# Signals and maxima of the maximum scores, per bank of two heads instead of per four heads

## The chip, the cores and the metric

The kernel runs on one core of a Trainium2 chip. The metric is the device time of one execution in microseconds (us), lower is better. A core has five engines that run their own instruction streams and meet only through semaphores: TensorE (PE; its weight loads are shown apart as PEld), VectorE (DVE), ScalarE (ACT), GpSimd (POOL) and SyncE (SP), which here issues all DMAs.

## The reference, cut to what matters

The kernel computes one block of a gated cross-attention network on x (4 x 2048 x 512) with a context of 154 tokens per batch item:

```python
x = x + tanh(g_xattn) * xattn(layernorm(x), ctx)      # 16 heads of 32, softmax over the 154 context tokens
x = x + tanh(g_ffn) * ffn(layernorm(x))               # 512 -> 2048 -> 512, relu, float_quantize of hidden, w2, out
```

Inside the attention, `att = q k^T / sqrt(32)`, a softmax over 154 columns, `y = att v`, and a projection by `Wo`. The softmax subtracts a maximum per row and head, and that maximum is what the change is about.

## The kernel before, in words

The 8192 rows of x are worked in 16 chunks of 512 rows (`CHUNK`), each with 4 tiles of 128 rows (`TILES`). The program is a software pipeline written out by hand: every stage has a table of beats (`MAX_AT`, `Q_AT`, `HIDDEN_AT`, ...), a chunk begins every 28 beats, and the first chunks have tables of their own (`MAX_OWN`, ...). Each engine walks over the same beats and issues, in a fixed order, its part of every stage that is due. Nothing is reordered at run time; each engine takes its stream in order.

The stages that matter here:

- **q projection** (`query`, L532, 12 matmuls `ring<-xT,wq`): PE writes one group of four heads (m = 0 to 3) to a ring bank of PSUM. DVE moves it out (`query_out`, L1091), ACT rounds it to f16 (`query_hi`, L883), POOL makes the low part (L1194).
- **rank** (PE, L638): for chunk c and u = 4m + t, two matmuls of 128 rows by 308 columns give the coarse scores of tile t against 154 keys of heads 4m to 4m+3. Each matmul covers two heads and fills one bank of the two-bank tile `m_ps` (for four early u of chunk 0, `PAIRED`, it is `s_ps`). Only the second signals `scored`. Before a rank, PE waits on `maxed` until the maximum of the rank before it has been taken, since both use the same two banks.
- **row_max** (DVE, L1048): one reduction over both banks, 616 columns to 4 maxima (`smax`), signals `maxed`.
- **shift** (DVE, L1054, L1059): after 8 ranks the maxima are scaled, rounded and transposed; SP writes them as an extra row of `qstack`, so that the exact scores come out shifted.
- **lift** (PE, L661 for the 26 left-over keys, L668 for the 128 main keys of a head): the exact scores, exponentiated twice by ACT (L834 as f16, L837 as f32); POOL forms the difference (L1182). `value` (L685 to L700) makes denominators and y.
- **projection, hidden layer, output** (L532 with `wo,yT` and `late_a,w`; L745): the bulk of PE's time. Between chunks, transposes of x run as DMAs on SP (L371, L381).

With 16 chunks of 16 ranks there are 256 ranks and 256 maxima. On PE the ranks stand singly between the 12-matmul products in the steady part, and close together while the pipeline fills. In the excerpt below, `rank` and `row_max` are the two sides; `keys_diagonal` (SP), `query_hi` (ACT) and `lift_ready` (PE) also wait on the two semaphores, and `shift` on `maxed`.

Of the kernel before, what the change touches and what calls it, by code (L numbers as in the profile page):

```python
# [10 lines left out]
ALU = mybir.AluOpType  # L11
ACT = mybir.ActivationFunctionType
AX = mybir.AxisListType
ABSMAX = bass.bass_isa.ReduceOp.absmax

P = 128
# [3 lines left out]
GH = P // DH  # L20
HID = 2048
HT = HID // P
TILES = 4
# [89 lines left out]
PAIRED = {(0, 1), (0, 3), (0, 5), (0, 7)}  # L113
# [3 lines left out]
def build(nc, x, ctx_t, g_xattn, g_ffn, wq_t, bq, wk_t, bk, wv_t, bv, wo_t, bo, w1_t, b1, w2_t, b2, out):  # L117
    NB, NK = ctx_t.shape[2], ctx_t.shape[3]
    NCH = x.shape[0] // CHUNK
    CPB = NCH // NB  # L120
# [3 lines left out]
    HK = 2 * NK  # L124
# [3 lines left out]
    with ExitStack() as es:  # L128
        def sb(name, shape, dt):
            return es.enter_context(nc.sbuf_tensor(name, shape, dt))  # L130

        def sem(name):
            return es.enter_context(nc.semaphore(name))
# [9 lines left out]
        kblk = sb("kblk", [P, KT, GH * NK], F16)  # L143
# [9 lines left out]
        qparts = sb("qparts", [P, 2, KT, CHUNK], F16)  # L153
# [19 lines left out]
        smax = sb("smax", [P, 2, 2 * GH, TILES], F32)  # L173
# [60 lines left out]
        def score_banks(c, u):  # L234
            return s_pair if (c, u) in PAIRED else m_ps
# [18 lines left out]
        q_done, q_moved, q_hi, q_lo = sem("q_done"), sem("q_moved"), sem("q_hi"), sem("q_lo")  # L254
        scored, maxed, negated, shifted = sem("scored"), sem("maxed"), sem("negated"), sem("shifted")
# [14 lines left out]
        ident_done, turned, turn_moved = sem("ident_done"), sem("turned"), sem("turn_moved")  # L270
# [65 lines left out]
        def unit(c, m, u):  # L336
            return group(c, m) * (GH + 1) + u

        def q_stage(c, m):
            if c:  # L340
                return q32[:]
            return (p32[:, 0, :], p32[:, 1, :], q32[:], y32[:])[m]
# [15 lines left out]
        def _(sp):  # L358
# [49 lines left out]
                    sp.dma_start(row[:, a], negT[32 * a:32 * a + 32, pair, :]).then_inc(shift_in[pair], DMA)  # L408

            def keys_diagonal(b, k):  # L410
                sp.wait_ge(scored, b * CPB * 16)
                if b == 2:
                    sp.wait_ge(kv_lo, EARLY + KT)
                for h in range(GH):
                    sp.dma_start(kblk[DH * h:DH * h + DH, :, h * NK:(h + 1) * NK],
                                 kst[DH * h:DH * h + DH, 0, :, b * NK:(b + 1) * NK]).then_inc(kblk_in, DMA)
# [87 lines left out]
            for beat in range(FIRST, (NCH - 1) * PERIOD + LAST):  # L504
                once(lambda pair: q_out(0, pair), QUERY_ROWS_AT, beat)
                once(lambda pair: q_in(0, pair), QUERY_ROWS_AT, beat)
                once(lambda b: values_stacked(b, 0), VALUE_ROWS_AT, beat)
                run(lambda c, t: x_load(c, t) if c > 1 else None, XLOAD_AT, beat)
                run(turn_x2, X2TURN_AT, beat, X2TURN_OWN)
                run(shift_row, SHIFT_AT, beat, SHIFT_OWN)  # L510
                run(lambda c, t: turn_x(c, t) if c else None, XTURN_AT, beat, XTURN_OWN)
                run(left_out, LEFT_AWAY_AT, beat)
                run(left_in, LEFT_BACK_AT, beat)
                run(reload, RELOAD_AT, beat, RELOAD_OWN)
                run_batch(keys_diagonal, KBLK_AT, beat)
                run_batch(values_stacked, VBLK_AT, beat)
                run(lambda c, pair: q_out(c, pair) if c else None, STACK_OUT_AT, beat, STACK_OUT_OWN)
                run(lambda c, pair: q_in(c, pair) if c else None, STACK_IN_AT, beat, STACK_IN_OWN)
                once(keys_out_all, KEYS_OUT_AT, beat)
                run_batch(keys_stacked, KST_AT, beat)  # L520
                run(store, STORE_AT, beat, STORE_OWN)
                once(w2_load, W2_LOAD, beat)
# [4 lines left out]
        def _(pe):  # L527
# [94 lines left out]
            def rank(c, u):  # L622
                m, t = divmod(u, TILES)
                pe.wait_ge(q_hi, c * KT + m + 1)
                if (c, u) == (0, 0):
                    pe.wait_ge(turn_moved, TILES)
                elif (c, u) == (0, 1):
                    pe.wait_ge(q_moved, 2)
                elif (c, u - 1) in PAIRED or (c, u) in PAIRED:
                    pe.wait_ge(maxed, c * 16 + u - 1)  # L630
                else:
                    pe.wait_ge(maxed, c * 16 + u)
                if c == 0 and u % 8 == 0:
                    pe.wait_ge(kblk_set[u // 8], GH)
                elif u == 0 and c >= CPB:
                    pe.wait_ge(kblk_in, c // CPB * GH * DMA)
                for half in range(2):
                    last = pe.matmul(score_banks(c, u)[:, half, 0:HK], qparts[:, 0, m, t * P:t * P + P],  # L638
                                     kblk[:, m, half * HK:(half + 1) * HK], start=True, stop=True)
                last.then_inc(scored, 1)  # L640

            def lift_ready(c, m, u):

                n = unit(c, m, u)
                if n >= 2:
                    pe.wait_ge(exped, n - 1)
                else:
                    pe.wait_ge(maxed, len(PAIRED) * 2)
                if m % 2 == 0 and u == 0:
                    pe.wait_ge(stack_in[m // 2], (c + 1) * 2 * STACK * DMA)  # L650
                    pe.wait_ge(shift_in[m // 2], (c + 1) * 4 * DMA)
                    if c < CPB:
                        pe.wait_ge(kcat_set, (m // 2 + 1) * GH)
                    else:
                        pe.wait_ge(kcat_in[m // 2], c // CPB * 2 * STACK * DMA)

            def lift_left(c, m):
                lift_ready(c, m, 0)
                dst = s_ps[unit(c, m, 0) % 2]
                for h in range(GH):  # L660
                    last = pe.matmul(dst[DH * h:DH * h + DH, :], kcat[0:97, GH * m + h, P:KW],  # L661
                                     qstack[0:97, GH * m + h, :], start=True, stop=True)
                last.then_inc(lifted, 1)
# [93 lines left out]
            for beat in range(FIRST, (NCH - 1) * PERIOD + LAST):  # L757
                run(lift_left, LEFT_AT, beat)
                run(value, VALUE_AT, beat)
                run(lift_main, MAIN_AT, beat)  # L760
                run(rank, MAX_AT, beat, MAX_OWN)
                once(stack_keys, KSTACK_AT, beat)
                steps_of(Q_STEPS, first_query, beat)
                steps_of(KV_STEPS, keys_values, beat)
                run(lambda c, m: query(c, m) if c else None, Q_AT, beat, Q_OWN)
                run(project, O_AT, beat, O_OWN)
                once(hidden_half, HIDDEN_HALVES, beat)
                run(lambda c, j: hidden(c, j) if c or j > 1 else None, HIDDEN_AT, beat, HIDDEN_OWN)
                run(ffn_out, FFN_AT, beat, FFN_OWN)

        @block.scalar
        def _(act):
# [105 lines left out]
            def query_hi(c, m):  # L878
                act.wait_ge(q_moved, c * KT + m + 1)
                if c:  # L880
                    act.wait_ge(scored, (c - 1) * 16 + 4 * m + 4)
                    act.wait_ge(stack_in[m // 2], c * 2 * STACK * DMA)
                nc.scalar.copy(qparts[:, 0, m, :], q_stage(c, m)).then_inc(q_hi, 1)  # L883

# [17 lines left out]
            for n in range(2):  # L902
                keys_values(n)
            query_hi(0, 0)
            first_blocks(0)
            query_hi(0, 1)
            for beat in range(FIRST, (NCH - 1) * PERIOD + LAST):
                run(exp_left, LEFT_AT, beat)
# [18 lines left out]
        def _(dve):  # L927
# [114 lines left out]

            def row_max(c, u):
                m, t = divmod(u, TILES)
                dve.wait_ge(scored, c * 16 + u + 1)
                heads = slice(m % 2 * GH, m % 2 * GH + GH)
                scores = score_banks(c, u)[:, :, 0:HK].rearrange("p a (h k) -> p a h k", h=2)
                nc.vector.tensor_reduce(smax[:, m // 2, heads, t].rearrange("p (a h) -> p a h", a=2), scores,  # L1048
                                        AX.X, ALU.max).then_inc(maxed, 1)

            def shift(c, pair):
                n = 2 * c + pair
                dve.wait_ge(maxed, c * 16 + 8 * pair + 8)
                nc.vector.tensor_scalar(neg16[:], smax[:, pair].rearrange("p h t -> p (h t)"), -1.0 / SHIFT, None, ALU.mult  # L1054
                                        ).then_inc(negated, 1)
                dve.wait_ge(negated, n + 1)
                if c:
                    dve.wait_ge(shift_in[pair], c * 4 * DMA)
                nc.vector.transpose(negT[:, pair, :], neg16[:]).then_inc(shifted, 1)  # L1059
# [254 lines left out]
```

## Time and profile before

| what | value |
|---|---|
| median of 3 runs | 1573.12 us (1571.85 to 1573.48) |
| the profiled execution | 1575.78 us, its span 1573.9 us |
| mean granted clock of TensorE in it | 0.992 |
| PE busy | 1528.2 us (97%), 8600 matmuls |
| DVE busy | 802.0 us (51%), 1299 instructions |
| ACT busy | 818.8 us (52%) |
| POOL busy | 879.2 us (56%) |

The profiled execution lies 2.66 us above the median of the runs; 1.9 us of it lie outside the span. Busy time is time in which at least one instruction of the engine was in flight. A matmul's shown duration is longer than the time until the next one may start, because matmuls are pipelined: what PE can do is read from the distance between starts. Slices of the span show PE at nine tenths or more from 160 us on; before that the pipeline fills and the weights are prepared.

### The profile page before, as it was taken

The numbers are of one execution on the slowest core, as the hardware profiler recorded it, in microseconds if no ns is written. First come the engines' busy times: TensorE is split into PE (matmuls) and PEld (weight loads), VectorE is DVE, ScalarE is ACT, GpSimd is POOL, SyncE is SP. The second block draws the span as 40 slices with busy tenths as digits, with TensorE's granted clock in tenths as the row PEclk, the third lists the DMA queues.
The fourth block names the chain that finished last, engine by engine and source line by source line (L and its number), as shares of the span: only waits on it lengthen the run. The fifth ranks groups of instructions, "written<-read, shape, count | busy, mean of one in ns | idle before, by whom it ended". The sixth has DMA issues, their size and how long they took to land.

```text
span 1573.9 us, 23573 instructions
## 1 busy us (share of the span) xinstructions
PE 1528.2 (97%) x8600; PEld 696.7 (44%) x8600; DVE 802.0 (51%) x1299; ACT 818.8 (52%) x1202; POOL 879.2 (56%) x919
## 2 busy tenths in 40 slices
PE   7877999999999999999999999999999999999998
PEld 4333444444444444444444444444444444444443
DVE  7777364555635455564645556464555646434221
ACT  5755755545455454545546454544645454455421
POOL 3778474654746465474646547464654747445310
PEclk9989999999999999999999999999999999999999
DMA  8446463454434353354444434344444434333120
GB/s 332 110 148 159 162 133 112 134 127 110 121 114 104 124 125 114 105 121 127 111 127 122 115 107 120 113 109 137 126 115 108 123 109 108 99 101 87 44 54 27
DMA packets 252854, 186.69 MB, mean 119 GB/s; under 512 B 160012, under 2 KB 209476, under 8 KB 251076
## 3 DMA queue, kind: packets, MB, share of 16 engines
q1 hardware_dynamic: 252740, 185.19, 42.7%
q8 instruction: 69, 1.13, 0.3%
q14 instruction: 45, 0.37, 0.1%
HBM read 99.95 MB, written 51.59 MB: 96 GB/s over the span
## 4 chain that ended last, share of the span: by engine, by line
PE 91%; SPq 2%; DVE 2%; DMA 2%; ACT 1%; issue 1%; POOL 1%; ACTq 0%; DVEq 0%
PE ring L532 62%; PE ring L745 14%; PE m_ps L638 4%; PE s_ps L668 3%; PE y_ps L696 2%; PE d_ps L685 2%; PE s_ps L661 1%; DMA resid<-in_wo_t 1%; PE y_ps L700 1%; PE d_ps L688 1%; SPq L371 1%; DVE smax L1048 0%; SPq L381 0%; PE ring L574 0%; ACT p L837 0%
## 5 line engine op out<-in xcount | busy, mean ns | idle before, releaser
L532 PE MATMUL ring<-late_a,w 128*128 128x512 f16 (+1 forms) x3096 | 703.9, 378 | 5.6 <-DMA late_a<-x 4.0
L532 PEld LDWEIGHTS ring<-late_a,w 128*128 128x128 f16 x3096 | 302.2, 98 | 346.2 <-issue 11.5
L859 ACT ACTIVATE late_b<-ring,b_sb,wsc 128x512 fp8e4<-128x512 f32 x256 | 199.3, 779 | 434.7 <-PE ring L532 434.7
L1182 POOL TENSOR_TENSOR pmain<-p,pmain 128x512 f16<-128x512 f32 x256 | 308.4, 1209 | 167.8 <-ACT p L837 167.6
L1048 DVE TENSOR_REDUCE smax<-m_ps 128x4 f32<-128x616 f32 x252 | 200.9, 797 | 244.7 <-PE m_ps L638 244.6
L837 ACT ACTIVATE p<-s_ps,prob_log,sc 128x512 f32<-128x512 f32 x320 | 248.0, 775 | 1.5 <-POOL pmain L1182 0.6
L745 PE MATMUL ring<-w,late_b 128*128 128x512 fp8e4 x1024 | 228.2, 379 | 0.9 <-ACT late_b L859 0.9
L834 ACT ACTIVATE pmain<-s_ps,prob_log,sc 128x512 f16<-128x512 f32 x256 | 198.3, 775 | 7.7 <-PE s_ps L668 7.7
L1182 POOL TENSOR_TENSOR pleft<-p,pleft 128x512 f16<-128x512 f32 x64 | 77.2, 1206 | 193.0 <-ACT p L837 192.8
L532 PE MATMUL ring<-wo,yT 128*128 128x512 f16 x768 | 174.5, 381 | 0.0
L532 PE MATMUL ring<-xT,wq 128*128 128x512 f16 x720 | 169.0, 385 | 2.2 <-DVE x L1030 2.2
L745 PEld LDWEIGHTS ring<-w,late_b 128*128 128x128 fp8e4 x1024 | 99.9, 98 | 122.3 <-ACT late_b L859 1.4
L1091 DVE TENSOR_SCALAR q<-ring,sc,bias_s 128x512 f32<-128x512 f32 x61 | 49.4, 810 | 171.1 <-PE ring L532 170.9
L1194 POOL TENSOR_TENSOR qparts<-q,qparts 128x512 f16<-128x512 f32 x61 | 72.6, 1190 | 96.6 <-ACT qparts L883 94.6
L638 PE MATMUL m_ps<-kblk,qparts 128*128 128x308 f16 x504 | 109.0, 298 | 16.2 <-DVE smax L1048 13.9
L532 PEld LDWEIGHTS ring<-wo,yT 128*128 128x128 f16 x768 | 74.1, 98 | 88.9 <-DVE resid L1114 5.7
L532 PEld LDWEIGHTS ring<-xT,wq 128*128 128x128 f16 x720 | 71.1, 99 | 83.7 <-issue 5.5
L1081 DVE TENSOR_TENSOR ffn<-ring,bq 128x512 f16<-128x512 f32 x64 | 44.1, 689 | 117.3 <-PE ring L745 117.3
L668 PE MATMUL s_ps<-qstack,kcat 97*128 97x512 f16 x256 | 95.6, 386 | 4.5 <-ACT p L837 4.4
L876 ACT CAST x<-xn 128x512 f16<-128x512 f32 x64 | 39.5, 617 | 114.9 <-DVE xn L1123 112.0
L1208 POOL TENSOR_TENSOR x<-xn,x 128x512 f16<-128x512 f32 x64 | 80.8, 1262 | 31.3 <-ACT x L876 31.2
L883 ACT CAST qparts<-q 128x512 f16<-128x512 f32 x61 | 37.7, 618 | 112.2 <-DVE q L1091 112.1
(158 smaller groups left out, 1452.7 us busy)
## 6 DMA issues: line engine op xcount, KB each, us to landing
qstack<-q_rows SPq DMA_DIRECT2D x192, 128.0 KB, 3.0
pstack<-left_rows SPq DMA_DIRECT2D x192, 128.0 KB, 2.6
xin<-in_x SPq DMA_DIRECT2D x64, 256.0 KB, 3.4
q_rows<-qparts SPq DMA_DIRECT2D x32, 512.0 KB, 2.8
left_rows<-pleft SPq DMA_DIRECT2D x64, 256.0 KB, 2.5
resid<-in_x SPq DMA_DIRECT2D x64, 256.0 KB, 3.2
out_x<-resid SPq DMA_DIRECT2D x64, 256.0 KB, 2.6
resid<-in_w_t SPq DMA_DIRECT2D x5, 1024.0 KB, 5.4
```

The lines of the kernel that those rows point to most:

```text
L532: last = pe.matmul(dst, lhs(a, k), rhs(b, k), start=(k == 0 and p == 0), stop=(k == n_k - 1 and p == 2))
L638: last = pe.matmul(score_banks(c, u)[:, half, 0:HK], qparts[:, 0, m, t * P:t * P + P], kblk[:, m, half * HK:(half + 1) * HK], start=True, ...
L668: pe.matmul(s_ps[unit(c, m, 1 + h) % 2], kcat[0:97, GH * m + h, 0:P], qstack[0:97, GH * m + h, :], start=True, stop=True).then_inc(lifted, 1)
L745: last = pe.matmul(ring_bank("f", c, t)[:], hT[:, j, t * P:t * P + P], w2[:, j, :], start=(j == 0), stop=(j == HT - 1))
L834: nc.scalar.activation(dst, s_ps[n % 2], ACT.Exp, bias=prob_log[:, 0:1], scale=sc[:, 7:8])
L837: nc.scalar.activation(p32[:, n % 2, :], s_ps[n % 2], ACT.Exp, bias=prob_log[:, 0:1], scale=sc[:, 7:8]).then_inc(exped, 1)
L859: nc.scalar.activation(hT[:, j, :], ring_bank("h", c, j)[:], ACT.Relu, bias=b1_sb[:, j:j + 1], scale=wsc[:, j // 4, 1:2], saturate=False). ...
L1048: nc.vector.tensor_reduce(smax[:, m // 2, heads, t].rearrange("p (a h) -> p a h", a=2), scores, AX.X, ALU.max).then_inc(maxed, 1)
L1091: nc.vector.tensor_scalar(q_stage(c, m), ring_bank("q", c, m)[:], sc[:, 6:7] if c else sc[:, 5:6], bias_s[:, m:m + 1], ALU.mult, ALU.add). ...
L1182: nc.gpsimd.tensor_tensor(part[:, 1, :], p32[:, n % 2, :], part[:, 0, :], ALU.subtract).then_inc(prob_lo, 1)
L1194: nc.gpsimd.tensor_tensor(qparts[:, 1, m, :], q_stage(c, m), qparts[:, 0, m, :], ALU.subtract).then_inc(q_lo, 1)
L1208: nc.gpsimd.tensor_tensor(x2_16[:, t % 2, 1, :], xn2[:], x2_16[:, t % 2, 0, :], ALU.subtract).then_inc(x2_split, 1)
```

## The change

The pair of matmuls of a rank now signals twice, once per bank, and DVE takes two maxima of 308 columns, each released by its own bank's signal, each signalling `maxed`. PE's first matmul of a rank waits for the first half of the maximum before it, the second matmul for the second half. All other waits on the two semaphores keep their meaning: their numbers are doubled.

```diff
@@ keys_diagonal (SP)
-                sp.wait_ge(scored, b * CPB * 16)
+                sp.wait_ge(scored, 2 * b * CPB * 16)
@@ rank (PE)
-                if (c, u) == (0, 0):
-                    pe.wait_ge(turn_moved, TILES)
-                elif (c, u) == (0, 1):
-                    pe.wait_ge(q_moved, 2)
-                elif (c, u - 1) in PAIRED or (c, u) in PAIRED:
-                    pe.wait_ge(maxed, c * 16 + u - 1)
-                else:
-                    pe.wait_ge(maxed, c * 16 + u)
...
                 for half in range(2):
-                    last = pe.matmul(score_banks(c, u)[:, half, 0:HK], qparts[:, 0, m, t * P:t * P + P],
-                                     kblk[:, m, half * HK:(half + 1) * HK], start=True, stop=True)
-                last.then_inc(scored, 1)
+                    if (c, u) == (0, 0):
+                        pe.wait_ge(turn_moved, TILES)
+                    elif (c, u) == (0, 1):
+                        pe.wait_ge(q_moved, 2)
+                    elif (c, u - 1) in PAIRED or (c, u) in PAIRED:
+                        pe.wait_ge(maxed, 2 * (c * 16 + u - 1) - 1 + half)
+                    else:
+                        pe.wait_ge(maxed, 2 * (c * 16 + u) - 1 + half)
+                    pe.matmul(score_banks(c, u)[:, half, 0:HK], qparts[:, 0, m, t * P:t * P + P],
+                              kblk[:, m, half * HK:(half + 1) * HK], start=True, stop=True).then_inc(scored, 1)
@@ lift_ready (PE)
-                    pe.wait_ge(maxed, len(PAIRED) * 2)
+                    pe.wait_ge(maxed, len(PAIRED) * 4)
@@ query_hi (ACT)
-                    act.wait_ge(scored, (c - 1) * 16 + 4 * m + 4)
+                    act.wait_ge(scored, 2 * ((c - 1) * 16 + 4 * m + 4))
@@ row_max (DVE)
-                dve.wait_ge(scored, c * 16 + u + 1)
-                heads = slice(m % 2 * GH, m % 2 * GH + GH)
-                scores = score_banks(c, u)[:, :, 0:HK].rearrange("p a (h k) -> p a h k", h=2)
-                nc.vector.tensor_reduce(smax[:, m // 2, heads, t].rearrange("p (a h) -> p a h", a=2), scores,
-                                        AX.X, ALU.max).then_inc(maxed, 1)
+                for half in range(2):
+                    heads = slice(m % 2 * GH + 2 * half, m % 2 * GH + 2 * half + 2)
+                    dve.wait_ge(scored, 2 * (c * 16 + u) + half + 1)
+                    nc.vector.tensor_reduce(smax[:, m // 2, heads, t],
+                                            score_banks(c, u)[:, half, 0:HK].rearrange("p (h k) -> p h k", h=2),
+                                            AX.X, ALU.max).then_inc(maxed, 1)
@@ shift (DVE)
-                dve.wait_ge(maxed, c * 16 + 8 * pair + 8)
+                dve.wait_ge(maxed, 2 * (c * 16 + 8 * pair + 8))
```

No instruction of PE moves; what changes there is which of them wait. PE, where the ranks of chunk 1 stand close together (`m_ps<-kblk,qparts` is a rank, `s_ps<-qstack,kcat` a lift), before:

```order
L668 MATMUL s_ps<-qstack,kcat 128x512 [waits exped]
L638 MATMUL m_ps<-kblk,qparts 128x308 [waits maxed,q_hi]
L638 MATMUL m_ps<-kblk,qparts 128x308
L638 MATMUL m_ps<-kblk,qparts 128x308 [waits maxed,q_hi]
L638 MATMUL m_ps<-kblk,qparts 128x308
```

The same place after the change:

```order
L667 MATMUL s_ps<-qstack,kcat 128x512 [waits exped]
L638 MATMUL m_ps<-kblk,qparts 128x308 [waits maxed,q_hi]
L638 MATMUL m_ps<-kblk,qparts 128x308 [waits maxed]
L638 MATMUL m_ps<-kblk,qparts 128x308 [waits maxed,q_hi]
L638 MATMUL m_ps<-kblk,qparts 128x308 [waits maxed]
```

Every second matmul of a rank now waits too. DVE at the same place (the rows behind the first are the three, then one, maxima of these ranks, with a layer-norm statistic between), before:

```order
L1107 TENSOR_SCALAR xin<-xin,mv,rs 128x512 [waits ln1_rs]
L1048 TENSOR_REDUCE smax<-m_ps 128x4 [waits scored] x3
L1097 BN_STATS bns<-xin 128x6 [waits ln1_stats,x_in2]
L1099 BN_AGGR mv<-bns 128x2 [waits ln1_bn]
L1048 TENSOR_REDUCE smax<-m_ps 128x4 [waits scored]
```

After the change:

```order
L1107 TENSOR_SCALAR xin<-xin,mv,rs 128x512 [waits ln1_rs]
L1047 TENSOR_REDUCE smax<-m_ps 128x2 [waits scored] x6
L1097 BN_STATS bns<-xin 128x6 [waits ln1_stats,x_in2]
L1099 BN_AGGR mv<-bns 128x2 [waits ln1_bn]
L1047 TENSOR_REDUCE smax<-m_ps 128x2 [waits scored] x2
```

Three maxima have become six and one has become two; nothing else stands elsewhere.

## Rows read from the trace of the kernel before

**Rows 1.** Who waited for whom on PE: us in total, times, longest

```profile
PE m_ps L638 <- DVE smax L1048: 13.9, 11, 3.4
```

**Rows 2.** Busy time by stretch: stretch, its length, then PE, PEld, DVE, ACT, POOL, clock, DMA

```profile
400.00:800.00 400.00, 400.00 (x2291) 181.75 (x2290) 212.15 (x340) 207.22 (x309) 239.27 (x251) 1.00 0.45 117
800.00:1200.00 400.00, 400.00 (x2319) 181.92 (x2318) 203.18 (x324) 212.53 (x317) 230.10 (x238) 1.00 0.43 118
```

**Rows 3.** Instructions on tile m_ps: count, ns min/median/max, first and last start

```profile
L638 PE MATMUL m_ps<-kblk,qparts x504: 291/295/462, 28.1 to 1414.7; 128*128 128x308 f16 x168
L1048 DVE TENSOR_REDUCE smax<-m_ps x252: 768/801/804, 28.5 to 1415.0; 128x4 f32<-128x616 f32 x126
```

**Rows 4.** Groups of instructions of DVE by shape: count, us in total, mean ns

```profile
L941 DVE TENSOR_REDUCE mag<-w 128x1 f32<-128x2048 f32 x1 | 2.3, 2286 | 0.0
```

**Rows 5.** Instructions of DVE in order of time: start us, duration us, instruction

```profile
40.00 0.95 DVE L1000 TENSOR_REDUCE kblk<-kst 32x308 f16<-32x308 f16 x2
...
830.79 0.79 DVE L1048 TENSOR_REDUCE smax<-m_ps 128x4 f32<-128x616 f32 x1
831.50 0.68 DVE L1097 BATCH_NORM_STATS2 bns<-xin 128x6 f32<-128x512 f32 x1
```

**Rows 6.** Instructions of PE in order of time, steady part, around 813 us

```profile
813.20 0.38 PE L668 MATMUL s_ps<-qstack,kcat 97*128 97x512 f16 x1
813.42 0.43 PE L638 MATMUL m_ps<-kblk,qparts 128*128 128x308 f16 x2
813.68 2.75 PE L532 MATMUL ring<-xT,wq 128*128 128x512 f16 x12
816.27 0.43 PE L638 MATMUL m_ps<-kblk,qparts 128*128 128x308 f16 x2
```

**Rows 7.** Instructions in order of time around 308 us, and the last such place

```profile
308.22 0.79 DVE L1048 TENSOR_REDUCE smax<-m_ps 128x4 f32<-128x616 f32 x1
308.79 0.38 PE L668 MATMUL s_ps<-qstack,kcat 97*128 97x512 f16 x1
309.15 0.42 PE L638 MATMUL m_ps<-kblk,qparts 128*128 128x308 f16 x2
...
1317.55 0.42 PE L638 MATMUL m_ps<-kblk,qparts 128*128 128x308 f16 x2
```

**Rows 8.** DVE, ACT and PE in order of time while the pipeline fills

```profile
105.00 0.79 DVE L1048 TENSOR_REDUCE smax<-m_ps 128x4 f32<-128x616 f32 x1
106.39 0.80 DVE L1048 TENSOR_REDUCE smax<-m_ps 128x4 f32<-128x616 f32 x1 [0.61 <-PE m_ps L638]
...
109.53 0.78 ACT L837 ACTIVATE p<-s_ps,prob_log,sc 128x512 f32<-128x512 f32 x1
...
105.93 0.42 PE L638 MATMUL m_ps<-kblk,qparts 128*128 128x308 f16 x2 [3.40 <-DVE smax L1048]
107.34 0.67 PE L638 MATMUL m_ps<-kblk,qparts 128*128 128x308 f16 x2 [0.98 <-DVE smax L1048]
109.00 0.67 PE L638 MATMUL m_ps<-kblk,qparts 128*128 128x308 f16 x2 [0.56 <-DVE smax L1048]
110.65 0.67 PE L638 MATMUL m_ps<-kblk,qparts 128*128 128x308 f16 x2 [0.56 <-DVE smax L1048]
...
111.55 5.28 PE L532 MATMUL ring<-xT,wq 128*128 128x512 f16 x12
116.66 0.43 PE L638 MATMUL m_ps<-kblk,qparts 128*128 128x308 f16 x2
```

**Rows 9.** Busy time by stretch, 110 to 115 us, columns as in the second group

```profile
110.00:115.00 5.00, 4.44 (x13) 1.65 (x13) 4.90 (x8) 4.87 (x6) 4.92 (x4) 0.50 0.10 32
```

**Rows 10.** The chain of work that ended last, in order of time: start us, us, what

```profile
39.29 0.79 DVE smax L1048
...
123.94 1.19 SPq L371
...
152.88 2.43 DMA late_a<-x
```

**Rows 11.** Instructions of PE in order of time, the last wait for a maximum

```profile
219.78 0.42 PE L638 MATMUL m_ps<-kblk,qparts 128*128 128x308 f16 x2 [0.98 <-DVE smax L1048]
```

## The prediction

> **What bounds the kernel now.** I read three views in this order. First the busy time by stretch: from 400 to 1200 us PE is busy without a gap at full granted clock, while DVE is busy half the time [rows 2]. In that part only what lies between two starts on PE counts. Second, who PE waited for: for the maxima it waited 13.9 us in 11 places, which is all this change can touch directly [rows 1]; the last of them is at 219.78 us [rows 11]. So the visible waits all belong to the filling of the pipeline. Third, the instructions in order of time, for waits too short to show as idle. One such repeats: at 308.79 us a lift of 512 columns starts, and the rank behind it starts 0.36 us later, where the same pair of rows is 0.22 us apart elsewhere [rows 6, 7]. The maximum before it ended at 308.22 + 0.79 = 309.01, and the rank follows by 0.14. That is a loss of 0.13 us per chunk, 12 times from 309.15 to 1317.55 [rows 7].
>
> **Prices.** PE's pair of 308 columns takes 0.26 us from start to next start, 0.13 per matmul [rows 6]. One matmul lasts 295 ns until its end is seen [rows 3]; DVE starts 0.46 us after the start of a pair (105.93 to 106.39), so 0.33 after that of its first matmul. PE starts 0.15 us after the end of a maximum (106.39 + 0.80 to 107.34) [rows 8].
> A maximum of 616 columns lasts 801 ns [rows 3], one of 2048 columns 2286 ns [rows 4]: (2286 - 801)/1432 = 1.04 ns a column and 0.16 us fixed. A half therefore lasts 0.16 + 308 x 1.04 ns = 0.48 us. Its successor starts 0.08 us before its end (830.79 + 0.79 against 831.50, [rows 5]), so two halves are about 0.39 us apart and both take 0.39 + 0.48 = 0.87 us, against 0.80. That is my value. The dearer end is the one pair of reductions of 308 elements in the trace: 0.95 us for two [rows 5]; with 0.48 for one they did not overlap, and both halves would take 0.95 to 0.98 us. It is another form (32 partitions, SBUF to SBUF), so I keep it for the range and take the overlap of the row on the same tile.
>
> **What a wait becomes.** Three cases.
> (a) DVE is late, PE's pair was finished long ago. Before, the next pair is through 0.80 + 0.15 + 0.26 = 1.21 us after DVE starts. After, the second matmul starts at 0.39 + 0.48 + 0.15 = 1.02 and is through at 1.15: 0.06 us won. The halves help little, since the second matmul waits for the second half, and PE had only 0.13 us to do in between. At the dearer end it is 0.05 lost.
> (b) DVE waits for PE. Before: 0.46 + 0.80 + 0.15 + 0.26 = 1.67 us from pair to end of the next pair. After: 0.33 + 0.39 + 0.48 + 0.15 + 0.13 = 1.48, so 0.19 won, 0.08 at the dearer end.
> (c) The same at half clock, where the pairs are 1.66 us apart [rows 8]: 0.47 for the pair instead of 0.26. Before 1.66 + 0.47 = 2.13; after 0.47 + 0.39 + 0.48 + 0.15 + 0.23 = 1.72, so 0.41 won; the lift between two pairs (0.43 at this clock) fits into the wait.
>
> **The filling, part by part.** The pair at 105.93 is case (a), 107.34 case (b), 109.00 and 110.65 case (c): 0.06 + 0.19 + 0.41 + 0.41 = 1.07 us. But the lift between 110.65 and 111.55 also waits for ACT, which ends an exponential at 109.53 + 0.78 = 110.31 [rows 8]; the product at 111.55 can then come no earlier than 110.31 + 0.15 + 0.43 = 110.89. So 0.66 us are left, and I take 0.7 with what a few earlier waits give. The product's end at 116.66 releases the chain that goes on, so this gain is kept. Waits behind it, up to 155 us, are worth nothing: from 123.94 us the chain is SP's queue of transposes and the DMA at 152.88 [rows 10]. The same holds before 66 us, except that a few maxima lie on the chain, the last of a row at 39.29 us [rows 10]: two of them each cost 0.07 more, a third, case (a) or (b), gives some back: +0.1 us. The wait at 219.78 [rows 11] is case (a): -0.06.
>
> **The steady part.** The 12 hidden waits are case (a): 12 x 0.06 = 0.7 us won, 0.6 lost at the dearer end. DVE gets 0.07 us more work per rank, 16 x 0.07 = 1.1 us in a chunk of 92 us with half of DVE idle [rows 2]: I cost it at nothing, its cover is that idle time; where it is missing (DVE late in front of something PE wants), it is 0.07 us a maximum. PE gets 256 more waits and 256 more signals. A lift has one of each: it takes 0.22 us, a matmul of the same width inside a product 2.59/12 = 0.216 [rows 6], so a wait with its signal costs 0 to 0.01 us; I take 0.004: 256 x 0.004 = 1.0 us, with 0 and 2.6 as ends. ScalarE's and SP's doubled counts change nothing.
>
> **Sum.** -0.7 (filling) + 0.1 (early chain) - 0.06 (219.78) - 0.7 (12 waits) + 1.0 (waits and signals) = -0.4 us, so 1575.4 us against the profiled execution's 1575.78. The median of the runs is 2.66 us lower: 1573.12 - 0.4 = 1572.7 us. A measurement of this kernel can tell about 0.2%, 3.1 us, from no change: I forecast no change.
>
> **A rule against the trace.** The maximum fits a fixed part of 0.16 us plus 1.04 ns a column, but its successor starts before its end [rows 3 to 5]. The Trainium skill, VectorE: DVE Perf Modes, section "The DRAIN you can't avoid", says that the next op does not start until the pipe is empty, and its rules for authors advise fewer ops. By that rule the two halves take 0.96 us, every case (a) turns into a loss of 0.03 us, and my sum would be +0.7. The trace disagrees for neighbours of this instruction: 0.71 us between starts at 0.79 us duration.
>
> **Rivals.**
> 1. *DVE becomes the bound of the filling* (slower). Mechanism: the second half starts only after the first has ended and the signal is back, and each maximum on DVE's stretches (100 to 116 us and around 40 us) delays what PE and the DMAs wait for. It decides against the change from 0.45 us between the halves on (then case (a) gains nothing). Price: 2 x 0.49 - 0.71 = 0.27 us more per maximum; if the 24 maxima of chunk 0's second half and chunk 1 all lie on the path, 6.5 us, with 12 x 0.05 of the steady part and 1 us of waits 8.1: 1581 us. For it: the 0.95 us row. Against: DVE waits for PE in most of these places, and the neighbours overlap. Chance 0.06 for more than 3.1 us.
> 2. *Every further signal holds PE up* (slower). Mechanism: the pair is no longer back to back. The widest reading of the rows is a tear as long as a round to the other engine, 0.15 us [rows 8], 256 x 0.15 = 38 us: 1611 us; the nearest row allows 0.01 us, 2.6 us. Against: lifts carry a wait and a signal each and follow at 0.22 us. Chance 0.05. The Trainium skill, TensorE: Matmul & The Clock Gate, section "The cost: per-tile semaphore tail", gives 26.3 ns for each further increment, one behind the other; as an estimate from that page it would be 256 x 26.3 ns = 6.7 us, 1578.4 us with the rest of my sum. No row here shows such a tail.
> 3. *The clock turns the filling* (faster). The product at 111.55 takes 5.11 us to 116.66 at half clock (granted 0.50, [rows 9]), 2.59 at full clock [rows 6], after PE had been idle 3.40 us at 105.93. If the shorter waits bring the clock back before it, 2.5 us more are won, 1573.12 - 0.4 - 2.5 = 1570.2 us; with one more such product in the filling, 1567.7. Against: the idle 3.40 us in front remain, only 0.1 us shorter. Chance 0.12, of which about 0.04 lie within 3.1 us. It can go the other way as well (a product pushed to half clock), with 2.5 us and 0.04 of chance, mostly within 3.1 us.
> 4. *It doesn't split anything*: excluded, since the order of the built program shows two reductions and two waits per rank.
>
> **How the numbers follow.** No change (sum -0.4) 0.73; rival 1 0.06 beyond the bound; rival 2 0.05; rival 3 0.12, and 0.04 for its mirror. Faster by over 0.2%: 0.08 of rival 3 and 0.02 for gains that I capped: 0.10. Slower by over 0.2%: 0.06 + 0.05 + 0.01 = 0.12. Within: 0.78. Range: the low end takes rival 3's first step, 1570.2; the high end all dearer ends, +0.1 + 0.05 + 0.6 + 2.6, with no gain in the filling: +3.35, 1576.5. I give 1570.2 to 1576.3.
>
> **What would show it.** Right: halves of 0.47 to 0.49 us, 0.39 apart where DVE is late; DVE busy up by 15 to 20 us; PE's waits for the maxima down from 13.9 to some 8 to 11 us; at the 12 places 0.30 us instead of 0.36 between lift and end of wait, or a small gap inside the pair; the pair still 0.26 to 0.27 us in the steady part; chunk period unchanged to 0.1 us. Wrong: pairs 0.30 us or longer everywhere (rival 2), halves 0.48 apart or more (rival 1), granted clock above 0.50 from 110 to 115 us (rival 3).

## The result, and the profile after

Before and after, run alternately on one chip: 1572.22 us median before (13 runs, 1568.03 to 1573.93), 1568.14 us after (13 runs, 1566.59 to 1571.01). The ratio is 0.9978 with a 95% interval of 0.997 to 0.9985: 3.5 us (2.4 to 4.7) faster, where gains in us, here and below, are worked out from the ratio and the median of before (the two medians alone differ by 4.1 us). The forecast was 0.4 us; the lower end of its range, 1570.2 us, lay 2.1 us above the 1568.14 us. Of these 2.1 us, 0.9 are the kernel before, whose median is now 1572.22 instead of the 1573.12 that the forecast started from: taken as a difference the lower end was 2.9 us faster, inside the interval of what was measured. The profiled execution of the change took 1567.14 us, its span is 1565.2 us.

The page after the change, its head and the engines' busy time:

```profile
span 1565.2 us, 23829 instructions
PE 1524.9 (97%) x8600; PEld 696.1 (44%) x8600; DVE 819.9 (52%) x1555; ACT 818.1 (52%) x1202; POOL 878.0 (56%) x919
```

DVE has 256 instructions more and 17.9 us more work, as costed (0.07 us for each of 256 maxima). The busy times of ACT and POOL stand as they did, to within 0.3%. Who PE waited for, after the change (us in total, times, longest):

```profile
PE m_ps L638 <- DVE smax L1047: 8.6, 9, 2.4
PE m_ps L638 <- issue: 2.6, 2, 2.4
```

The 13.9 us of [rows 1] have become 8.6 in the row for the maxima; 2.6 more are put down to nothing, so the row alone says little of what was won. The instructions on tile m_ps after the change (count, ns min/median/max, first and last start):

```profile
L638 PE MATMUL m_ps<-kblk,qparts x504: 291/295/457, 27.4 to 1406.0; 128*128 128x308 f16 x168
L1047 DVE TENSOR_REDUCE smax<-m_ps x504: 447/471/483, 27.8 to 1406.6; 128x2 f32<-128x308 f32 x168
```

A half takes 471 ns, forecast 480 ns from the fit through [rows 3, 4].

**The steady part.** The clearest measure is the distance between chunks. The transposes of the denominators on DVE come four to a chunk; the first one of chunk 3 and the first one of chunk 14 are 11 chunks apart. Before:

```profile
326.76 0.70 DVE L1068 STREAM_TRANSPOSE y<-d_ps 128x512 f32<-128x512 f32 x1
1335.16 0.70 DVE L1068 STREAM_TRANSPOSE y<-d_ps 128x512 f32<-128x512 f32 x1
```

After:

```profile
319.58 0.70 DVE L1068 STREAM_TRANSPOSE y<-d_ps 128x512 f32<-128x512 f32 x1
1326.52 0.70 DVE L1068 STREAM_TRANSPOSE y<-d_ps 128x512 f32<-128x512 f32 x1
```

1008.40/11 = 91.67 us before, 1006.94/11 = 91.54 us after, and each of the eleven distances is within 0.01 us of its mean. So 0.13 us a chunk are won, all of the hidden wait of [rows 7], 12 x 0.13 = 1.6 us. From the first transpose of chunk 14 to the end it is 238.7 us in all fourteen profiles of this document, so what else differs between two of them lies in the filling. The same place after the change, in order of time:

```profile
301.17 0.85 DVE L1047 TENSOR_REDUCE smax<-m_ps 128x2 f32<-128x308 f32 x2
301.75 0.38 PE L667 MATMUL s_ps<-qstack,kcat 97*128 97x512 f16 x1
301.97 0.43 PE L638 MATMUL m_ps<-kblk,qparts 128*128 128x308 f16 x2
302.08 0.10 PEld L638 LDWEIGHTS m_ps<-kblk,qparts 128*128 128x128 f16 x1 [0.23 <-DVE smax L1047]
302.24 2.75 PE L532 MATMUL ring<-wo,yT 128*128 128x512 f16 x12
```

The two halves end at 301.17 + 0.85 = 302.02, 0.85 us after they began, 0.06 more than one whole maximum took. The rank follows the lift by 0.22 us, without a wait; the second matmul's weights are loaded at 302.08, 0.06 us after the second half, and the next product comes 0.27 us after the pair, as anywhere. Reckoned with the 0.15 us of the forecast, the second matmul would have come at 302.17.

**The filling** went 7.2 us faster in this pair of profiles (326.76 to 319.58). That is more than the runs bear out: the profiled execution of before (1575.78 us) took longer than any of the 13 runs. What repeats in other profiles is told below.

### The profile page after: what moved, and what is told of

Read it like the earlier page. It is cut to its first block, busy times and chain, and to the rows that moved or that the text cites. A ratio compares the mean times of both kernels' runs of the same rounds, so it can differ in the third digit from the quotient of the medians.

```text
span 1565.2 us, 23829 instructions
## 1 busy us (share of the span) xinstructions
PE 1524.9 (97%) x8600; PEld 696.1 (44%) x8600; DVE 819.9 (52%) x1555; ACT 818.1 (52%) x1202; POOL 878.0 (56%) x919
## 4 chain that ended last, share of the span: by engine, by line
PE 92%; DVE 2%; DMA 2%; SPq 1%; ACT 1%; POOL 1%; issue 1%; ACTq 0%; DVEq 0%
PE ring L532 62%; PE ring L744 14%; PE m_ps L638 4%; PE s_ps L667 3%; PE y_ps L695 3%; PE d_ps L684 2%; PE s_ps L660 1%; DMA resid<-in_wo_t 1%; PE y_ps L699 1%; PE d_ps L687 1%; DVE smax L1047 0%; PE ring L574 0%; ACT p L836 0%; PE ring L592 0%; ACT pmain L833 0%
## 5 line engine op out<-in xcount | busy, mean ns | idle before, releaser
L1047 DVE TENSOR_REDUCE smax<-m_ps 128x2 f32<-128x308 f32 x504 | 217.2, 473 | 219.4 <-PE m_ps L638 218.9
L1203 POOL TENSOR_TENSOR x<-xin,x 128x512 f16<-128x512 f32 x60 | 69.2, 1154 | 48.0 <-ACT x L867 48.0
```

Of the source, the lines that this page charges most:

```text
L1047: nc.vector.tensor_reduce(smax[:, m // 2, heads, t], score_banks(c, u)[:, half, 0:HK].rearrange("p (h k) -> p h k", h=2), AX.X, ALU.max).t ...
L1203: nc.gpsimd.tensor_tensor(x16[:, t % 2, 1, :], xin[:, t, :], x16[:, t % 2, 0, :], ALU.subtract).then_inc(x_split, 1)
```

## The experiments

The kernels were timed in three groups of four (1 to 4, 5 to 8, 9 to 12), each group alternately with the kernel before on one chip. In the diffs, `split(c)` says whether chunk c works by halves, and `signals(n)` is the number of signals of the first n ranks.

**1 and 2: halves in the steady part alone, halves in the filling alone.** The change, but `split` true for chunks 3 to 15, or for chunks 0 to 2:

```diff
+        def split(n):
+            return n >= 3        # e2: n < 3
...
                 for half in range(2):
+                    if half == 0 or split(c):
... (the waits of the change, counted with signals)
-                last.then_inc(scored, 1)
+                    if half or split(c):
+                        last.then_inc(scored, 1)
```

(against the kernel before, PE's side; DVE takes two maxima where `split(c)` holds). Where a chunk is not split, the rank and its maximum are those of before, but for one rank: the first one behind a split chunk, (3, 0) in e2 and (1, 0) in e10 below, waits for the first half of the maximum before it alone, for both its matmuls. To be safe it would have to wait for both halves; it is one rank of 256.

> Theory A (the halves take away waits on PE: 12 hidden ones of 0.13 us in the steady part, the shown ones in the filling; waits and signals themselves cost nothing): with halves only from chunk 3 on, the 12 places vanish, the distance between chunks is 91.54 us instead of 91.67, and the total is 1.6 us lower (ratio 0.999). Theory B (the gain is all in the filling, where the granted clock and the queue of transposes happen to fall better): no change, ratio 1.000, distance between chunks 91.67 us.

> Halves only in chunks 0 to 2. Theory A: the rest of the gain, some 2 to 2.5 us (ratio 0.9985), distance between chunks as before the change, 91.67 us. Theory B: the whole gain, 3.5 to 4 us (ratio 0.9976).

Measured: e1 0.9989 (0.998 to 0.9998), 1.7 us faster, distance between chunks 91.54 us. e2 0.9993 (0.9983 to 1.0003), 1.1 us faster, 91.67 us. So theory B falls: about half of the gain is the steady part, and it is the hidden waits. The gain of e2 is not clear of zero (2.7 us faster to 0.5 slower). The two add up to 2.8 us; the full change was measured three times, at 3.5, 2.8 and 3.3 us.

**3: PE waits for the whole maximum.** From the full change (in its own counts, the ranks around `PAIRED` likewise):

```diff
-                        pe.wait_ge(maxed, 2 * (c * 16 + u) - 1 + half)
+                        pe.wait_ge(maxed, 2 * (c * 16 + u))
```

> Both signals and both maxima in all chunks, but PE's first matmul of a rank waits for the whole maximum before it. Theory A (what pays is that the first matmul needs only the first half): the two maxima take 0.05 to 0.06 us longer than one, so the 12 hidden waits grow from 0.13 to about 0.19 us and the distance between chunks to about 91.72 us; the filling keeps only what DVE wins by starting 0.13 us earlier; total between 0.5 us slower and 1 us faster. Rival C (what pays is DVE's earlier start): nearly the whole gain, ratio 0.998.

Measured: 1.0014 (1.0005 to 1.0023), 2.2 us slower (0.8 to 3.6); from the starts at 325.39 and 1334.46 us the distance between chunks is 91.73. The hidden wait, in order of time:

```profile
306.78 0.85 DVE L1058 TENSOR_REDUCE smax<-m_ps 128x2 f32<-128x308 f32 x2
307.36 0.38 PE L677 MATMUL s_ps<-qstack,kcat 97*128 97x512 f16 x1
307.78 0.42 PE L646 MATMUL m_ps<-kblk,qparts 128*128 128x308 f16 x2
```

Lift to rank is 0.42 us instead of 0.36: the 0.06 us by which two halves take longer, as theory A had it for the steady part. In twelve chunks that makes 0.7 us. The total is worse than theory A's 0.5 us, so some 1.5 us are lost in the filling; no run shows by what. Rival C falls in any case: DVE's earlier start by itself is not what pays.

**4: both maxima start late.**

```diff
-                    dve.wait_ge(scored, 2 * (c * 16 + u) + half + 1)
+                    dve.wait_ge(scored, 2 * (c * 16 + u) + 2)
```

> Both signals and both maxima, PE waits by halves, but both maxima wait for the second matmul of the rank. Theory A: the steady part as with the full change (DVE is late there anyway), distance between chunks 91.54 us, 1.6 us; in the filling each wait in which DVE waits for PE gives 0.06 us instead of 0.19, so 0.5 to 1 us less than the full change: total 2.5 to 3.5 us lower. Rival C: the gain goes, ratio 1.000.

Measured: 0.9982 (0.9973 to 0.9991), 2.8 us faster, distance between chunks 91.54 us. As theory A had it. With experiment 3 it shows that the first matmul's earlier release carries the whole gain of the steady part (91.73 to 91.54 us) and most of the total (3 and 4 differ from the full change by one edit each).

**5: the price of signals and waits.** PE's side alone; DVE takes one maximum:

```diff
                 for half in range(2):
+                    if half and c * 16 + u > 1:
+                        pe.wait_ge(maxed, c * 16 + u - (1 if (c, u - 1) in PAIRED or (c, u) in PAIRED else 0))
-                    last = pe.matmul(score_banks(c, u)[:, half, 0:HK], qparts[:, 0, m, t * P:t * P + P],
-                                     kblk[:, m, half * HK:(half + 1) * HK], start=True, stop=True)
-                last.then_inc(scored, 1)
+                    pe.matmul(score_banks(c, u)[:, half, 0:HK], qparts[:, 0, m, t * P:t * P + P],
+                              kblk[:, m, half * HK:(half + 1) * HK], start=True, stop=True).then_inc(scored, 1)
...
-                dve.wait_ge(scored, c * 16 + u + 1)
+                dve.wait_ge(scored, 2 * (c * 16 + u + 1))
```

> PE's side of the change alone: each matmul of a rank signals, the second one waits too (for the same whole maximum as the first, so it never holds), DVE takes one maximum as before. The term of the sum says 0.004 us a rank: distance between chunks 91.67 + 16 x 0.004 = 91.73 us, total +1.0 us. Theory A' (a satisfied wait and a signal cost nothing): 91.67 us, ratio 1.000. Rival 2 of the prediction as the page's figure has it, 26 ns a signal: 92.09 us, +6.7 us.

Measured: 1.0003 (0.9992 to 1.0013), and the two transposes:

```profile
323.32 0.70 DVE L1069 STREAM_TRANSPOSE y<-d_ps 128x512 f32<-128x512 f32 x1
1331.65 0.70 DVE L1069 STREAM_TRANSPOSE y<-d_ps 128x512 f32<-128x512 f32 x1
```

1008.33/11 = 91.67 us. 16 further signals and 16 further satisfied waits a chunk cost less than 0.01 us together. The 1.0 us of the sum was nothing. The program has no instruction more either: its page counts 23573 instructions, as before.

**6: one semaphore instead of two in front of a rank.** From the kernel before:

```diff
-                pe.wait_ge(q_hi, c * KT + m + 1)
+                if t == 0:
+                    pe.wait_ge(q_hi, c * KT + m + 1)
```

(at t > 0 PE has already waited for the same value at t = 0).

> The kernel before with one edit: PE waits for the rounded queries only at the first tile of a group, so a rank at t > 0 waits for one semaphore instead of two. Theory D (a second semaphore in front of a matmul makes it start some 0.05 us later once the maximum is there; this is why the hidden waits vanished wholly): the 12 hidden waits fall from 0.13 to 0.08 us, distance between chunks 91.62 us, total 0.6 us lower. If the number of semaphores does not matter: 91.67 us and 1.000.

Measured: 0.999 (0.9976 to 1.0004), distance between chunks 91.59 us, 0.08 less than before. The hidden wait:

```profile
303.65 0.79 DVE L1066 TENSOR_REDUCE smax<-m_ps 128x4 f32<-128x616 f32 x1
304.23 0.38 PE L678 MATMUL s_ps<-qstack,kcat 97*128 97x512 f16 x1
304.49 0.11 PEld L647 LDWEIGHTS m_ps<-kblk,qparts 128*128 128x128 f16 x2 [0.38 <-DVE smax L1066]
304.50 0.44 PE L647 MATMUL m_ps<-kblk,qparts 128*128 128x308 f16 x2
```

The maximum ends at 304.44, PE starts 0.06 us later, not 0.14 as in [rows 7]. Theory D holds, and with more than it asked: a second semaphore in front of the matmul costs 0.08 us at the moment of release. The page counts 23381 instructions, 192 fewer than before, one for each rank at t > 0: a second wait on a matmul is an instruction of its own, a single one is not. Whether the order of the two waits matters was not tried. The whole kernel's gain of 1.6 us (interval to 0.6 us slower) can't be told from the 0.08 x 12 = 1.0 us that this makes.

**7 and 8: the full change with that edit, and the full change again.**

> The full change with the same edit. In the steady part nothing is left to win: 91.54 us. By theory D each of the some ten waits of the filling gets up to 0.05 us shorter: 0 to 0.5 us below the full change, ratio to before 0.9975 to 0.998.

> The full change once more, with the numbers of the semaphores computed by a function and the same instructions and waits: distance between chunks 91.54 us, 3 to 4 us below before, ratio 0.9978; beside it the other runs of this call can be read.

Measured: e7 0.9993 (0.9981 to 1.0005), e8 0.9982 (0.9971 to 0.9992), both 91.54 us between chunks. Theory D's further gain did not show; e7 lies 1.7 us above e8, none of it in the steady part, and its waits for the maxima are shorter (7.7 us against 8.4). The intervals of the two overlap, so it isn't shown that e7 is worse; shorter waits in the filling did at least not bring a filling that is shorter by their amount.

**9 to 12: which chunks of the filling.** `split(n)` as `n >= 1`; as `n == 0`; `n >= 1` with the single wait from chunk 1 on; and the full change a third time.

> Halves from chunk 1 on; the ranks before 74 us are as before the change. In the traces so far, every kernel whose early ranks are released sooner shows half clock from 66.5 to about 70 us behind the wait for pstack, and its second denominator transpose comes 0.7 to 1.9 us later than the first, against before; in the kernels with chunk 0 as before it does not. Theory E (that dip is caused by the shorter waits of chunk 0, whose gain is hidden behind SP's queue anyway, and costs 1 us): full clock from 62 to 72 us, the gain at 100 to 117 us kept, total 1 us below the full change, ratio to before 0.9972. If the early shift does not matter in the end: as the full change, 0.998.

> Halves in chunk 0 alone. Theory E: granted clock 0.83 or lower from 62 to 72 us, nothing won, total 0.5 to 1 us above before, ratio 1.0003 to 1.0007, distance between chunks 91.67 us. If the dip has another cause: ratio 1.000 and clock 1.00.

> As the kernel with halves from chunk 1, and from chunk 1 on PE waits for the rounded queries only at the first tile of a group. Theory D gives up to 0.3 us more than that kernel (ratio 0.9970); the earlier kernel with the single wait everywhere was 1 to 2 us worse than the full change, which theory D does not explain: if this one is worse too, shorter waits in the filling are not worth what they take off.

> The full change once more beside these: ratio to before 0.998, clock below 1.00 from 62 to 72 us, distance between chunks 91.54 us.

| kernel | ratio to before (95%) | median us | granted clock, 62 to 72 us |
|---|---|---|---|
| e9, halves from chunk 1 | 0.9970 (0.9959 to 0.9981) | 1567.20 | 1.00 |
| e10, chunk 0 only | 1.0007 (0.9997 to 1.0016) | 1572.53 | 1.00 |
| e11, from chunk 1, one wait | 0.9969 (0.9956 to 0.9983) | 1567.85 | 1.00 |
| e12, the full change | 0.9979 (0.9967 to 0.9990) | 1568.24 | 0.83 |

Chunk 0 gives nothing that shows, so the filling's gain comes from chunks 1 and 2. Between e9 and e11 the single wait makes no difference, so the loss that e7 seemed to have is not repeated. The ratios stand in the order that theory E gave, with its sizes, but their intervals overlap, and e10's clock speaks against it: its early ranks are released as in the full change, PE waits 1.85 us for `pstack`, and it ran on at full clock. Busy time of two stretches of 2 us (stretch, length, PE, PEld, DVE, ACT, POOL with their instructions, PE's granted clock, share of DMA, GB/s); first the change, whose PE had idled 1.89 us before 65.92 us,

```profile
66.00:68.00 2.00, 2.00 (x28) 0.80 (x27) 1.13 (x3) 0.62 (x2) 2.00 (x3) 0.69 0.44 68
68.00:70.00 2.00, 2.00 (x8) 0.94 (x5) 1.25 (x2) 0.00 (x0) 1.35 (x2) 0.50 0.50 22
```

then e10, idle 1.85 us before 66.05:

```profile
66.00:68.00 2.00, 1.95 (x29) 1.04 (x30) 1.00 (x3) 0.78 (x2) 2.00 (x3) 1.00 0.28 55
68.00:70.00 2.00, 1.69 (x8) 0.71 (x6) 1.97 (x4) 1.22 (x2) 1.53 (x2) 1.00 0.74 49
```

Nine profiles have the release of the maxima changed in chunk 0, and in eight of them the clock fell to half here, in e10's not; in the five with chunk 0 as before it fell in none. The length of this one idle stretch does not tell the two apart: half clock came with 1.39 us (e3), 1.43 (e6) and 1.65 to 1.89 us, full clock with 1.36 to 1.49 us (before, e1, e5, e9, e11) and 1.85 us (e10). In the change, 0.69 and 0.50 over 4 us leave 1.6 us of full clock ungranted. Whether e9 is really better than the full change is open; it is not worse.

## Why the prediction was wrong

**What held.** PE is the bound of the steady part and DVE's extra work is hidden there. The size of a half (0.471 for 0.48 us), the overlap (0.85 for 0.87 us for both), the 12 hidden waits, and that PE waits there for a late maximum. Rivals 1 and 2 did not come: the halves overlap, and 256 signals cost nothing. The rule that was set against the trace had been read too widely: the same section of the Trainium skill (VectorE: DVE Perf Modes, "The DRAIN you can't avoid") goes on that a next op that is not held starts earlier, and the trace agrees: two halves of 0.47 us take 0.85 us together. Three steps failed, two in the steady part and one in the filling.

**Step 1, "the second matmul starts at 0.39 + 0.48 + 0.15 = 1.02".** The 0.15 us from the end of a maximum to PE was read on ranks that wait for two semaphores. The second matmul of a rank waits for `maxed` alone, and follows by 0.06 us (302.02 to 302.08). Experiment 6 shows the same on its own: 0.06 instead of 0.14 us, 91.59 instead of 91.67. With it, case (a) wins 0.06 + 0.09 = 0.15 us instead of 0.06, more than the 0.13 that there was: 1.6 us instead of 0.7. Case (b) wins 0.28 instead of 0.19: the wait of [rows 11] was one of these (the pair before it started at 218.37 and the maximum 0.46 us later), not case (a) as I had put it. Before, 220.04 - 218.37 = 1.67 us from that pair to the end of the next; after:

```profile
211.63 0.43 PE L638 MATMUL m_ps<-kblk,qparts 128*128 128x308 f16 x2
212.59 0.60 PE L638 MATMUL m_ps<-kblk,qparts 128*128 128x308 f16 x2 [0.53 <-DVE smax L1047]
213.02 1.24 PE L532 MATMUL ring<-wo,yT 128*128 128x512 f16 x5
```

213.02 - 211.63 = 1.39 us (the view ends at 214 us, within the product).

What neither the forecast nor the change touches is why DVE is late there. Before the change, around the hidden wait of [rows 7]:

```profile
306.85 1.16 POOL L1182 TENSOR_TENSOR pmain<-p,pmain 128x512 f16<-128x512 f32 x1
306.92 1.37 DVE L1107 TENSOR_SCALAR xin<-xin,mv,rs 128x512 f32<-128x512 f32 x1 [2.80 <-POOL rs L1220]
```

The last step of the layer norm takes 1.37 us, 0.52 at 319.26 us, and only then comes the maximum, at 308.22. So it is in all 12 places: 1.37 us, begun 0.07 us after the start of an instruction of POOL's on pmain and ended 0.28 us after that one's end. With 0.52 us, as an estimate, the maximum would end 0.85 us earlier, before the lift even starts, and the change would have nothing to win in the steady part. No kernel was made that tries it.

**Step 2, "a wait with its signal costs 0.004 us".** The term of 1.0 us was mis-sized: it came from a difference of two rounded starts (0.22 against 0.216), and experiment 5 measures nothing. Both steps together: forecast +0.3 us for the steady part, measured -1.6 (experiment 1: -1.7). That is 1.9 of the 3.1 us by which I was off; the other 1.2 are the filling. With these two steps right the sum would have been -2.3 us, 1570.8 us, inside the range.

**Step 3, the filling: "0.66 us are left, this gain is kept".** Forecast -0.7; the three measurements of the full change less 1.6 leave 1.2 to 1.9 us, experiment 2 has 1.1 (0.5 slower to 2.7 faster). The mechanism was partly another one. In order of time, after the change:

```profile
102.75 0.62 DVE L1107 TENSOR_SCALAR xin<-xin,mv,rs 128x512 f32<-128x512 f32 x1
103.30 1.81 DVE L1047 TENSOR_REDUCE smax<-m_ps 128x2 f32<-128x308 f32 x4
...
101.10 0.43 PE L638 MATMUL m_ps<-kblk,qparts 128*128 128x308 f16 x2
103.91 0.66 PE L638 MATMUL m_ps<-kblk,qparts 128*128 128x308 f16 x2 [2.38 <-DVE smax L1047]
104.86 0.73 PE L638 MATMUL m_ps<-kblk,qparts 128*128 128x308 f16 x2 [0.29 <-DVE smax L1047]
...
109.06 3.79 PE L532 MATMUL ring<-xT,wq 128*128 128x512 f16 x12
112.69 0.43 PE L638 MATMUL m_ps<-kblk,qparts 128*128 128x308 f16 x2
```

From the first of the four waits to the product: 109.06 - 103.91 = 5.15 us, before 111.55 - 105.93 = 5.62 [rows 8], 0.47 won of the 0.66 that were reckoned with. But two more things moved. The long wait in front is 1.0 us shorter (2.38 for 3.40), where the forecast had 0.1. About 0.3 of it is that PE needs only the first half of the maximum; the rest is the layer norm's last step on DVE, which takes 0.62 us; before it took 1.40:

```profile
103.63 1.16 POOL L1182 TENSOR_TENSOR pleft<-p,pleft 128x512 f16<-128x512 f32 x1
103.68 1.40 DVE L1107 TENSOR_SCALAR xin<-xin,mv,rs 128x512 f32<-128x512 f32 x1
```

Both start within 0.05 us of each other, and DVE's ends 0.29 us after POOL's (105.08 and 104.79). POOL's instructions after the change:

```profile
101.93 1.16 POOL L1177 TENSOR_TENSOR vmain<-x,vmain 128x512 f16<-128x512 f32 x1
103.05 1.34 POOL L1182 TENSOR_TENSOR pleft<-p,pleft 128x512 f16<-128x512 f32 x1
```

DVE now comes in time to end 0.28 us after the instruction before that, on vmain (103.37 and 103.09), and POOL's on pleft takes longer, 1.34 us for 1.16. In the nine profiles where PE waits for the maxima of chunk 1 by halves or through one semaphore the step takes 0.54 to 0.62 us. In the five others it takes 1.40 to 1.53, starts within 0.09 us of POOL's instruction on pleft and ends 0.28 or 0.29 us after it. The Trainium skill, SBUF — State Buffer, "Who interferes with whom", has VectorE share one pair of ports with GpSimd under an exclusive lock. The rows agree as far as they go: DVE's instruction ends 0.28 us after one of POOL's.

And the product after the four ranks takes 3.63 us to the next rank instead of 5.11: part of it runs at full clock again. That is rival 3, which I had at 0.12, in part. Busy time from 102 to 118 us (the columns of [rows 2]), before, after, and in experiment 3:

```profile
102.00:118.00 16.00, 9.58 (x28) 3.10 (x26) 12.68 (x20) 11.87 (x15) 14.26 (x14) 0.68 0.42 135
102.00:118.00 16.00, 10.72 (x61) 3.80 (x61) 13.22 (x26) 14.40 (x18) 15.40 (x15) 0.79 0.52 161
102.00:118.00 16.00, 8.97 (x48) 3.09 (x41) 14.42 (x28) 13.50 (x18) 14.28 (x14) 0.79 0.50 161
```

The clock has two levels, so 0.68 is 10.2 us at half clock in these 16, and 0.79 is 6.8. The four profiles in which chunk 1 is as before (before, e1, e5, e10) all have 0.68, the ten others all 0.79. The stretch from the fourth q to the fifth (DVE's rows `q<-ring`) takes 16.99 us before; it is 2.1 to 2.6 us shorter in the nine profiles above and 0 to 0.3 in e1, e5 and e10. Experiment 3 has the shorter half clock without the shorter step on DVE:

```profile
104.80 1.52 DVE L1124 TENSOR_SCALAR xin<-xin,mv,rs 128x512 f32<-128x512 f32 x1
...
112.62 3.36 PE L538 MATMUL ring<-xT,wq 128*128 128x512 f16 x12
115.82 0.43 PE L646 MATMUL m_ps<-kblk,qparts 128*128 128x308 f16 x2
```

Its product takes 3.20 us and its stretch is 1.6 us shorter. So most of what this stretch wins is the clock, and not the step on DVE; what brings the clock back sooner is not shown.

Only part of this reaches the end, contrary to "this gain is kept". Behind it the chain runs over SP's queue and DMAs [rows 10], and this passage varies by 3 us between profiles of kernels that are the same up to there: from the fourth q at 99.87 us to the seventh at 168.58 it is 3.0 us shorter in e1, which fills the pipeline exactly as before, and e3 with its shorter stretch is slower in all. How the 1.1 to 1.9 us of the filling divide among waits, clash with POOL, clock and DMA queue stays open.

**The chances.** "No change" had 0.78 and "faster by over 0.2%" 0.10. Of the two, the second came, if by little: 0.22%, with an interval that reaches from 0.15 to 0.3. Two figures of the forecast are off by a little, and nothing hangs on it: the high end adds up to 1576.5 us and is given as 1576.3, and the sum by the rule against the trace comes to +0.8 us where +0.7 stands.

## What to carry to other kernels

Where an engine waits for a buffer of two banks, release it bank by bank, and ask which part lets the first waiting instruction go: here the first matmul's wait paid, and splitting the work without splitting that wait was slower (experiment 3). Look first at why the other engine is late: here it was one instruction that took 1.37 us instead of 0.52. Read a release latency from an instruction that waits for as many semaphores as the one you cost, and take a redundant wait away in front of it. In a pipeline's steady part use the distance between repeats over many of them: it shows 0.01 us, where the whole run shows 1 to 2 us.

## What the runs showed of the hardware that was not expected

- A TensorE instruction that waits for two semaphores follows the releasing VectorE instruction by 0.14 us, one that waits for one by 0.06 us (experiment 6 and the second matmul of the change). The Trainium skill, Perfetto Trace Analysis, "Identifying Dependency Chains", notes that instructions waiting on multiple engines may have extra semaphore instructions inserted before them; the trace agrees, with 192 instructions fewer for 192 second waits taken away. Its price here is 0.08 us.
- 256 further increments and 254 satisfied waits on TensorE (experiment 5) cost less than 0.01 us per 16. The Trainium skill (TensorE: Matmul & The Clock Gate, "The cost: per-tile semaphore tail") states 26.3 ns an increment for a tail behind tiles that each signal; between matmuls that follow one another on the whole array these runs show nothing of it.
- An idle stretch of 1.4 to 1.9 us in front of the first denominators came with half clock in eight profiles; with 1.36 to 1.49 us in five others and 1.85 us in one the clock stayed at full (0.50 to 0.69 against 1.00).
- The same VectorE instruction (128x512, f32, SBUF to SBUF) took 0.54 to 0.62 us or 1.40 to 1.53 us; in the long form it began within 0.09 us of the start of one of GpSimd's and ended 0.28 to 0.29 us after that one's end. In the steady part it took 1.37 us once a chunk.
